# A cross-attention and expert kernel: V kept on chip in four homes, rows of K and Q copied inside SBUF, and the first key projection cut by contraction halves

## What is computed

```python
def _L0_xattn_ref(x, mem, W_kv, W_q, W_proj, b_proj):
    kv = (mem @ W_kv).reshape(B, Nkv, 2, HEADS, HEAD_DIM)
    k = kv[:, :, 0].transpose(0, 2, 1, 3)
    v = kv[:, :, 1].transpose(0, 2, 1, 3)
    q = (x @ W_q).reshape(B, Nq, HEADS, HEAD_DIM).transpose(0, 2, 1, 3)
    attn = jnp.einsum('bhqd,bhkd->bhqk', q, k) * SCALE
    attn = jax.nn.softmax(attn, axis=-1)
    out = jnp.einsum('bhqk,bhkd->bhqd', attn, v)
    out = out.transpose(0, 2, 1, 3).reshape(B, Nq, C)
    return out @ W_proj + b_proj
...
x = x + jnp.tanh(g_xattn[0]) * _L0_xattn_ref(_layernorm(x), ctx_1024, W_kv, W_q, W_proj, b_proj)
x = x + jnp.tanh(g_ffn[0]) * _L0_ffn_ref(_layernorm(x), gate_w, w_up, w_down, sg_gate, sg_up, sg_down)
```

## Time and profile before

| what | us |
|---|---|
| three runs | 525.05, 526.12, 528.61 |
| median | 526.12 |
| profiled execution | 525.73 |
| its span | 524.0 |
| PE busy | 500.8 (96%) |
| DVE busy | 296.0 (56%) |
| ACT busy | 271.5 (52%) |
| POOL busy | 172.0 (33%) |
| bytes moved by DMA | 58.60 MB |

### The profile page before, as it was taken

One profiled execution on the slowest core, in us unless ns is written; L12 is line 12 of the kernel. 1 busy time (PEld: TensorE's weight loads), 2 busy tenths in 40 slices (PEclk: granted clock), 3 DMA queues, 4 the chain that ended last, 5 costly groups with the idle time before them and its releaser, 6 DMA issues.

```text
span 524.0 us, 8546 instructions
## 1 busy us (share of the span) xinstructions
PE 500.8 (96%) x2972; PEld 315.1 (60%) x2972; DVE 296.0 (56%) x538; ACT 271.5 (52%) x435; POOL 172.0 (33%) x193
## 2 busy tenths in 40 slices
PE   8989899999999999999989999999999999999992
PEld 6645433333333333334456466599999999999991
DVE  3765778877887788884565697133333333333321
ACT  1656277777777777775554303105444444444430
POOL 4400176772211111111000002104566666655642
PEclk9999999999999999999999999999999999999997
DMA  7999419977773666300003001222433334444432
GB/s 252 307 289 282 166 65 243 255 181 213 201 182 95 171 172 171 82 1 23 0 27 136 1 0 54 68 80 44 69 60 63 62 61 64 66 65 69 61 43 30
DMA packets 44882, 58.60 MB, mean 112 GB/s; under 512 B 6352, under 2 KB 36688, under 8 KB 44336
## 3 DMA queue, kind: packets, MB, share of 16 engines
q1 hardware_dynamic: 29536, 36.12, 25.2%
q0 software_dynamic: 7488, 10.23, 12.7%
q10 hardware_dynamic: 7824, 11.81, 7.0%
HBM read 37.89 MB, written 20.05 MB: 111 GB/s over the span
## 4 chain that ended last, share of the span: by engine, by line
PE 78%; DMA 9%; DVE 5%; issue 2%; ACT 2%; SPq 2%; POOLq 1%; POOL 0%; DVEq 0%
PE ps L1105 62%; PE ps L1191 11%; DMA out<-unit_region 5%; DMA x_sb<-in_x 2%; PE ps L1199 2%; PE ps L1477 1%; DVE neg_max L824 1%; ACT ctx_region L675 1%; DMA unit_region<-nm_parts 1%; DMA unit_region<-qk_parts 1%; SPq L344 1%; PE ps L1308 1%; DVE stats L775 1%; DVE rows L789 1%; SPq L363 0%
## 5 line engine op out<-in xcount | busy, mean ns | idle before, releaser
L824 DVE TENSOR_REDUCE neg_max<-ps 128x2 f32<-128x1024 f32 x128 | 151.2, 1219 | 42.2 <-PE ps L1105 41.8
L675 ACT ACTIVATE ctx_region<-ps 128x512 f32<-128x512 f32 x256 | 139.9, 595 | 57.9 <-PE ps L1105 57.7
L1105 PE MATMUL ps<-unit_region 96*128 96x512 bf16 (+1 forms) x512 | 133.2, 381 | 4.9 <-DMA unit_region<-qk_parts 1.8
L1105 PE MATMUL ps<-unit_region,ctx_region 128*128 128x128 f32 (+1 forms) x968 | 113.8, 274 | 0.0
L1105 PEld LDWEIGHTS ps<-unit_region,ctx_region 128*128 128x128 f32 (+1 forms) x968 | 110.5, 189 | 0.6 <-issue 0.3
L1105 PEld LDWEIGHTS ps<-unit_region 96*128 96x128 bf16 (+1 forms) x512 | 48.2, 98 | 97.7 <-ACT ctx_region L675 59.1
L562 POOL DMA_INDIRECT out<-unit_region x39 | 61.9, 1586 | 55.5 <-DMA out<-unit_region 52.4
L1105 PE MATMUL ps<-dn_region,unit_region 128*128 (+1 forms) x330 | 78.2, 379 | 0.0
L535 POOL DMA_INDIRECT unit_region<-x_rows,unit_region x39 | 38.7, 991 | 118.7 <-DVE unit_region L1059 81.6
L740 ACT COPY ctx_region<-up_region 128x1536 f32 x39 | 57.3, 1472 | 34.7 <-PE ps L1105 31.8
L1191 PE MATMUL ps<-ctx_region,unit_region 128*32 128x512 f32 x512 | 68.2, 604 | 2.2 <-ACT ctx_region L675 0.7
(11 more groups left out here) (152 smaller groups left out, 408.5 us busy)
## 6 DMA issues: line engine op xcount, KB each, us to landing
up_region<-in_w_upT ACTq DMA_DIRECT2D x9, 768.0 KB, 4.5
qk_parts<-up_region SPq DMA_DIRECT2D x32, 192.0 KB, 3.2
unit_region<-qk_parts SPq DMA_DIRECT2D x32, 192.0 KB, 4.5
v_rows<-dn_region SPq DMA_DIRECT2D x4, 1024.0 KB, 5.8
unit_region<-qk_parts SPq DMA_DIRECT2D x32, 128.0 KB, 4.5
unit_region<-v_rows SPq DMA_DIRECT2D x16, 256.0 KB, 5.4
dn_region<-in_w_downT ACTq DMA_DIRECT2D x9, 384.0 KB, 5.6
ctx_region<-in_ctxT SPq DMA_DIRECT2D x4, 512.0 KB, 11.2
```

Source lines behind the costliest of these rows:

```text
L675: nc.scalar.activation(probs[:, k % 8, :], bank(4 + k % 2), ACT.Exp).then_inc(exp_done, 1)
L824: nc.vector.tensor_reduce(neg_max[:, s, 2 * p:2 * p + 2], bank(2 * (p % 2), 2), AX.X, ALU.max, negate=True).then_inc(max_done, 1)
L1105: return nc.tensor.matmul(o_, w, m, start=start, stop=stop)
```

## The change

1. `v_sb` with two homes becomes `v_home(b)` with four, one per batch: homes 0 and 1 where `v_sb` lay, home 2 over `resid`, home 3 at the end of `unit_region` where `v_unit` was. ACT copies V there and PE reads it there. The DRAM tensor `v_rows`, its stores and loads and their semaphores are gone. The ones are written by four memsets instead of one.
2. The DRAM tensor `qk_parts` is gone. `load_rows` copies each part's 64 rows of a unit from `parts` straight to `k_unit` or `q_unit`, in twelve DMAs of 64 KB per unit.
3. SP's order: K's rows of units 0 and 1 as soon as K of batch 0 is split, then Q's.
4. The first key projection runs over the two halves of the contraction, each with its own DMAs and semaphore (`k_half`), and `WARM` falls from 36 to 26.
5. PE's and ACT's loops over the slots are unrolled; DVE's stays.
6. The weights' loads are spread by `UP_AT` and `DOWN_AT`, guarded by `unit_in` of the batch whose parts lie there (`PARTS_READ`).
7. PE's wait for `whole_sb` moves from ahead of slot 0 to its `turn_max`.

```diff
-WARM = 36
+WARM = 26
-K_RUNS = ((0, 1, 2), (0,), (0, 1))
-Q_RUNS = ((0, 1), (0, 1, 2), (0,))
+K_PARTS = (0, 1, 2, 0, 0, 1)
+Q_PARTS = (0, 1, 0, 1, 2, 0)
+PARTS_READ = {2: 0, 5: 1, 9: 2, 13: 3}
+UP_AT = (2, 3, 5, 6, 9, 10, 13, 14, 7)
+DOWN_AT = (13, 14, 15, 5, 6, 9, 10, 11, 1)
...
+        V_AT = (2 * DC * T, 2 * DC * T + v_words, 0)
+
+        def v_home(b):
+            home = (dn_region[:, V_AT[b]:V_AT[b] + v_words] if b < len(V_AT) else unit_region[:, 4 * HG * T:unit_words])
+            return home.rearrange("p (k h w) -> p k h w", k=TB, h=H)
...
-            sp.dma_start(wkv_sb[:, :, 0:D], w_kv_rows[:, :, 0:D]).then_inc(wk_in, 16)
-            load_ctx(0)
+            for d in range(DC):
+                sp.dma_start(wkv_sb[:, d, 0:D], w_kv_rows[:, d, 0:D]).then_inc(k_half[d], 16)
+                sp.dma_start(ctx_sb[:, d, 0:T], ctxT[d * P:(d + 1) * P, 0:T]).then_inc(k_half[d], 16)
...
-            def load_rows(b, g, a, dst, runs):
-                row = 0
-                for run in runs:
-                    n = len(run)
-                    src = qk_parts[a, bass.ds(b, 1), g, 0:n, :, :].rearrange("a j (d h) n -> (a j d) (h n)", h=HG)
-                    to = dst[row:row + n * HD, g, :, :].rearrange("p h n -> p (h n)")
-                    sp.dma_start(to, src).then_inc(unit_in[g], 16)
-                    row += n * HD
+            def load_rows(b, g, a, dst, order):
+                half = P // 2 * (g % 2)
+                for i, j in enumerate(order):
+                    sp.dma_start(dst[i * HD:(i + 1) * HD, g, :, :], parts[half:half + P // 2, b, a, j, g // 2, :]
+                                 ).then_inc(unit_in[g], 16)
...
-            send_k(0)
-            send_v(0)
-            send_q(0)
-            sp.wait_ge(k_out[0], 16 * QK_OUTS)
+            sp.wait_ge(low_done, QK_ORDER.index((1, 0)) + 1)
             for g in range(2):
-                load_rows(0, g, 1, k_unit, K_RUNS)
-            sp.wait_ge(q_out[0], 16 * QK_OUTS)
+                load_rows(0, g, 1, k_unit, K_PARTS)
+            sp.wait_ge(low_done, QK_ORDER.index((0, 0)) + 1)
             for g in range(2):
-                load_rows(0, g, 0, q_unit, Q_RUNS)
...
+            for u in range(1, UNITS):
+                if u in PARTS_READ:
+                    for g in range(NG):
+                        act.wait_ge(unit_in[g], 16 * LOADS * (PARTS_READ[u] + 1))
+                if u in UP_AT:
+                    load_up(UP_AT.index(u))
+                if u in DOWN_AT:
+                    if u > NG:
+                        act.wait_ge(pv_done, (u - 1) // NG * NG * TB)
+                    load_down(DOWN_AT.index(u))
                 exp_slot(u, u % NG, more_max=u + 1 < UNITS)
...
+            def first_k():
+                for d in range(DC):
+                    pe.wait_ge(k_half[d], 16 * 2)
+                    for c in range(DC):
+                        last = mm(bank(K_BANK + c), wkv_sb[:, d, c * P:(c + 1) * P], ctx_sb[:, d, 0:T], d == 0, d == DC - 1)
+                last.then_inc(k_ps, 1)
```

More of the change, by code:

```diff
@@ L244, in build @@
         ctx_in = [sem(f"ctx_in{b}") for b in range(B)]
-        wk_in, wv_in, wq_in = sem("wk_in"), sem("wv_in"), sem("wq_in")
+        k_half = [sem(f"k_half{d}") for d in range(DC)]
+        wv_in, wq_in = sem("wv_in"), sem("wq_in")
         gates_in = sem("gates_in")
@@ L273, in build @@
         split_step, split_done = sem("split_step"), sem("split_done")
-        k_out = [sem(f"k_out{b}") for b in range(B)]
-        v_out = [sem(f"v_out{b}") for b in range(B)]
-        q_out = [sem(f"q_out{b}") for b in range(B)]
         unit_in = [sem(f"unit_in{s}") for s in range(4)]
-        v_in = [sem(f"v_in{s}") for s in range(4)]
         pair_ps = sem("pair_ps")
@@ L406, in _ @@
                     send_max(u + 1, (g + 1) % NG)
-                    if 1 <= u <= len(SPLIT_ORDER):
-                        a, late = SPLIT_ORDER[u - 1]
-                        send_parts(a, late, k_out[late] if a else q_out[late])
-                    if g == 0:
-                        sp.wait_ge(k_out[b], 16 * QK_OUTS)
-                        sp.wait_ge(q_out[b], 16 * QK_OUTS)
-                        sp.wait_ge(v_out[b], 16)
+                    if b == 1:
+                        sp.wait_ge(low_done, len(QK_ORDER) // 2)
+                    elif g == 0:
+                        for a in range(2):
+                            sp.wait_ge(split_done, SPLIT_ORDER.index((a, b)) + 1)
                     sp.wait_ge(pv_done, u * TB + TB)
@@ L681, in _ @@
             exp_slot(0, 0, first=True)
-            for b in range(B):
-                act.wait_ge(v_out[b], 16)
-            for b in range(B - 1):
-                for late in ((0, 1), (2,), (3,))[b]:
-                    act.wait_ge(k_out[late], 16 * QK_OUTS)
-                    act.wait_ge(q_out[late], 16 * QK_OUTS)
-                for r in range(1, NG + 1):
-                    if r < NG:
-                        load_expert(b * 3 + r - 1)
-                    exp_slot(b * NG + r, r % NG)
-            for u in range(UNITS - 3, UNITS):
+            for u in range(1, UNITS):
[8 more added lines that the diff above has]
+                    load_down(DOWN_AT.index(u))
                 exp_slot(u, u % NG, more_max=u + 1 < UNITS)
@@ L1190, in pv @@
                 for h in range(HG):
[L1191 removed]
+                    last = nc.tensor.matmul(bank(6)[h * VW:(h + 1) * VW, :], v_home(u // NG)[:, kt, u % NG * HG + h, :],
                                             probs[:, (kt * HG + h) % 8, :], start=kt == 0, stop=kt == TB - 1,
@@ L1236, in slot @@
                             pe.wait_ge(nmT_sb, 1)
+                            pe.wait_ge(whole_sb, len(WHOLE_ORDER))
                         else:
@@ L1245, in _ @@
             TURN_MAX, TURN_OUT = 3, 9
-            for b in range(2):
-                project_k(b, 0)
-                project_k(b, 1)
+            def first_k():
[4 more added lines that the diff above has]
+                last.then_inc(k_ps, 1)
+            for b in range(2):
+                if b == 0:
+                    first_k()
+                else:
+                    project_k(b, 0)
+                    project_k(b, 1)
                 project_v(b, (0, 1))
@@ L1299, in _ @@
             pe.wait_ge(ones_rows, 1)
+            pe.wait_ge(v_ones, B)
             pe.wait_ge(rowsT_sb, B)
-            pe.wait_ge(whole_sb, len(WHOLE_ORDER))
             slot(0, 0, 0, first=True)
-            with pe.Fori(0, B - 1) as b:
-                for r in range(1, NG + 1):
-                    slot(b * NG + r, b, r)
+            for u in range(1, UNITS - 3):
+                slot(u, (u - 1) // NG, (u - 1) % NG + 1)
             def turn_attn(t):
```

75 lines of the change are left out of this document (20 added, 55 removed).

## The result

| | before | changed |
|---|---|---|
| time, median of 4 runs, us | 525.72 (525.05 to 528.61) | 543.68 (541.22 to 546.52) |
| profiled execution: span, us | 524.0 | 544.7 |
| busy time of PE, us | 500.8 | 506.7 |
| data moved, MB | 58.60 | 43.99 |

The changed kernel takes 1.033 times as long (95% interval 1.027 to 1.040). 523.5 was forecast, with a range up to 530.5: the forecast was wrong. A quarter less data is moved, and the kernel is slower by 18 us. (A fourth run of the kernel before, 525.32, puts its median at 525.72 in place of 526.12.)

A forecast was written before the change was run, and what follows sets the result against it. PE was taken as the bound, busy 500.8 of 524.0 us. Span: 524.0 - 2.8 - 0.6 - 0.2 - 0.6 + 1.2 + 0.4 = 521.4; the same 2.6 us off the median 526.12 gave 523.5 us, range 520 to 530.5.

The forecast's parts named there:

- the term of the slots: Twelve exposed slots, units 2 to 13: SP's twelve copies delay the maxima, 0.1 us late each, 1.2 us lost.
- rival 3: SP becomes the bound: a copy costs above 0.64 us, each further 0.01 us costing 1.4 us; chance 0.2.
- The start: Before the first slot: no DRAM between and an earlier first projection together gain 2.8 us, error about 1 us.
- Rows without DRAM: At the start, K and Q rows copied directly: PE's 1.8 us wait for unit 0's rows goes.
- The divided loads: First key projection on half loads after ten fewer warming transposes: PE starts 1.1 us earlier.
- the signs: List of what would show the forecast right; among them, the first slot starts 4 us earlier.
- rival 4: The start gives nothing: x1 lands 1 to 2 us later or PE idles between halves; 525 to 526.5; chance 0.05.
- First slot: Slot 0: the `whole_sb` wait now stands after two scores, so ACT's first exponential follows L625 at once; 0.6 us gained.
- unrolling, slot of unit 4: PE's unrolled batch loop gains 0.2 us at two inner ends; unit 4's late slot, its queue emptied, gains 0.6 us.

The follow-up runs named there:

- the one wait changed: Changed kernel, with SP's copies of a unit's rows waiting for the unit's last scores (`score_ps`) instead of its last P.V (`pv_done`): 523.45 us, ratio 0.997.

## Why the prediction was wrong, step by step

- **The step that failed** is the term of the slots: "in some of them weights are in the queue, so I take 0.1 us late each, 1.2 us lost". The slots lost 22.7 us against the same slots without a wait (181.1 against 158.4), and 21.7 against the kernel before, where the sum had + 0.4 in all (1.2 - 0.2 - 0.6). The working before it was sound: a copy at 0.63 us against 0.62 taken, maxima of 1.86 against 1.79, landing 1.8; an ordinary slot is late by 0.2, where 0.07 stood for such a pace. What was wrong is that everything that disturbs the queue entered as a tenth. Six groups of copies have one that is 0.6 to 1.2 us longer, beside an instruction DMA, which the prediction does not have at all; and late maxima met the weight loads. The sum came out 0.05 us early in a slot, so any disturbance would be paid in full, and that could have been seen from what stood there. (Expectations of later runs put the longer copies down to the weight loads; the traces do not bear that out.)
- **Late maxima meet the weight loads.** ACT issues its loads when it enters a slot. As long as the maxima are issued before that, they land in 1.8 us (0.2 us ahead was enough); late by a microsecond, which in all three cases is that of a long copy, they land beside 768 to 1152 KB, after 4.2 to 5.3. The price jumps where it was drawn as a straight line (rival 3's 1.4 us for each 0.01 us of a copy). Weight loads were moved to other slots, and I priced their issue on ACT alone (0.4 us; the end behind the fourteenth transpose grew by 0.2), not what flies beside them.
- **The clock.** PE's clock was 1.00 in every stretch that I used, and I took it as given. Behind waits of over 3 us stand three stretches near 0.50, which cost about 5.5 us.
- **Rival 3** had the right place and the right sign, with a chance of 0.2, but its condition, a copy above 0.64, did not come: 0.634 lies in the forecast's own 0.60 to 0.64. It was priced by the copy's cost alone; at 0.634 its arithmetic (1.4 us for each 0.01 over 0.62) gives 525.5. The releaser that was to show it was DMA of `nm_parts`; the profile printed "issue", and only the spacing (12.44 and more) and the waits of PE showed it.
- **The start** was to give 2.8 us. The third pair of scores came at 38.47 in place of 36.25 (before 39.03): 0.6. Two parts lay in the term. Rows without DRAM do give about what was worked out: first transpose 2.7 us earlier in the kernel with them and the undivided start, 0.0 with DRAM. The divided loads took 1.3 back. The first half was there in time (issued at 1.25, landed 5.2 later), but PE came to it at 6.94 and not at 6.5: ten transposes were priced at 0.11 us each, 1.1, and 26 took 5.53 us where 36 had taken 6.01. The second half was there at 9.6, not 8.3, and V's weight at 12.5. (The sum has 2.8 + 0.6 = 3.4 us for the first slot, where the signs say 4.) And x of batch 1, which I took as hidden behind 11.53 us of queue, was 1.6 us later. PE in the changed kernel, then DVE's first statistics of batch 1 (before: 14.61):

```profile
6.94 1.88 PE L1064 MATMUL ps<-ctx_region,wkv_sb 128*128 128x512 f32 x4
9.62 1.98 PE L1064 MATMUL ps<-ctx_region,wkv_sb 128*128 128x512 f32 x4 [0.80 <-DMA ctx_region<-in_ctxT]
12.51 1.99 PE L1064 MATMUL ps<-wkv_sb,ctx_region 128*128 128x256 f32 x8 [0.90 <-DMA wkv_sb<-in_w_kv]
```

```profile
16.25 1.41 DVE L734 BATCH_NORM_STATS2 stats<-x_sb 128x6 f32<-128x256 f32 x4 [2.27 <-DMA x_sb<-in_x]
```

  That is rival 4's case, foreseen with 0.05. I had reckoned with 277 GB/s, the mean from 2 to 5 us; there it is 268 now, but from 4 to 5 us it was 214, where the kernel before had 383:

```profile
4.00:5.00 1.00, 1.00 (x6) 1.00 (x6) 0.29 (x1) 0.00 (x0) 0.19 (x2) 1.00 0.78 214
```

  I had turned a stretch's rate into arrival times of single loads, as if the queue in question were served first.
- **First slot** and **unrolling, slot of unit 4**: 0.7 us against 0.6, and 1.1 (159.3 to 158.3) against 0.8. Both were right.

With the one wait changed, the kernel's 521.7 us of span stand beside the 521.4 that the sum gave. That is luck in part, for part by part they differ: its first transpose is 2.1 us later than forecast (64.69 against 66.02 - 3.4), its slots 1.3 shorter and its end 0.4.

## What to carry to other kernels

Where several transfers of one queue have one deadline, add their issue times and the last landing from the moment at which the first may start, and compare with the time there is; a sum that fits by 0.05 us has no room for one long issue, and the step over the edge is not small, since late transfers meet others and long waits cost clock. If it does not fit, look first at what the queue waits for: a wait that guarded a buffer which the change has taken away can be replaced by the one that still holds. And when a step is moved on a queue, list every wait that reads its result: the copies were needed two slots earlier than their use in the products suggests.

## What the runs showed of the hardware

- SP issues a copy of 64 KB from 64 partitions into 16 every 0.63 us, and twelve take 7.6 us, also with 1152 KB of weights under way (7.61, the run with the weight loads later, at 140.92). One that runs beside a DMA of 16 KB of the queue "instruction" can take 1.0 to 1.9 us: in the fourteen traces 71 of the 72 DMA issues of SP over 0.9 us, from 60 to 245 us, begin within 0.8 us of the start of such a DMA. Whose instructions it brings, and why SP's issue is longer beside it, was not tried. The Trainium skill ("DMA: Bandwidth & Descriptors") says in its rules for kernel authors to join small transfers; here the price of the copies was neither their bandwidth nor their landing (2.6 us), but their issue on one queue.
- A DMA of 4 KB lands 1.8 us after its issue, where nothing else flies, and 4.2 to 5.3 us after where a load of 768 KB on the other queue is issued from 0.62 us ahead of it to 0.15 behind it (four cases, in the changed kernel and with the start undivided); where such a load comes 0.19 us or more behind it, it is 1.7 to 1.8 again. In the kernel before, with rows on their way through DRAM, it is up to 5.1 us in some slots, and ready in time. Whether it is the load's size or its shape was not separated.
- 48 small DMAs issued by GpSimd lengthen the end of the program by 2.0 us, in three kernels alike (10.3 against 8.3), though the last of them is issued about 280 us earlier.
- One load divided in two by contraction halves (four DMAs for two) brought its second half 2.0 us later than the undivided load brought the whole (9.62 against 7.64), and delayed loads behind it by 1.3 to 1.6 us.
